# Query stack rows of a pair in a transfer of 48 rows and one of 24, and stack rows dealt to other partitions

## What is computed

```python
q = (x1 @ Wq + bq).reshape(Bn, Nq, H, D).transpose(0, 2, 1, 3)
k = concatenate([x2 @ Wk + bk, memory_k], axis=1)      # 128 + 120 keys
v = concatenate([x2 @ Wv + bv, memory_v], axis=1)
attn = softmax(einsum('bhqd,bhkd->bhqk', q, k) * D ** -0.5)
out = einsum('bhqk,bhkd->bhqd', attn, v)
return x + out.transpose(0, 2, 1, 3).reshape(Bn, Nq, C) @ Wp + bp
```

## Time and profile before

| | us |
|---|---|
| runs of before | 1510.54, 1493.03, 1508.12 |
| median | 1508.12 |
| the profiled execution, its time | 1501.2 |
| its span, first to last instruction | 1499.5 |
| layer 0's attention | some 5 to 540 |
| expert tiles | some 540 to 920 |
| layer 1's attention | some 930 to 1270 |
| adapter | to the end |

### The profile page before, as it was taken

How to read it: one execution, slowest core, us unless ns; L and a number is a source line. 1 busy time by engine, 2 the same in 40 slices (tenths; PEclk the granted TensorE clock), 3 DMA queues, 4 the chain that set the end, 5 groups by cost and what they waited for, 6 DMA issues and landing times. The chain is left out here.

```text
span 1499.5 us, 45714 instructions
## 1 busy us (share of the span) xinstructions
PE 1305.9 (87%) x16549; PEld 1075.4 (72%) x16549; DVE 1078.4 (72%) x3442; ACT 840.7 (56%) x1570; POOL 831.6 (55%) x992
## 2 busy tenths in 40 slices
PE   1799999999999994699999997379999999889998
PEld 0378787778777773699999986157777777666776
DVE  6779989999989975355444444478888788567775
ACT  1267677777777772455555553146666655534444
POOL 4356888888888746466666665345544443022220
PEclk9899999999999996799999999579999999979999
DMA  5666777767777614122222222789998896122221
GB/s 171 222 196 217 238 229 235 233 205 238 231 232 227 211 33 174 54 60 61 57 59 59 61 57 63 182 232 257 253 261 255 256 256 215 60 69 64 75 79 43
DMA packets 183988, 239.26 MB, mean 160 GB/s; under 512 B 37745, under 2 KB 147185, under 8 KB 176609
## 3 DMA queue, kind: packets, MB, share of 16 engines
q1 hardware_dynamic: 164608, 209.51, 45.2%
q0 software_dynamic: 13024, 25.91, 7.1%
q10 hardware_dynamic: 6144, 1.06, 0.4%
HBM read 148.34 MB, written 87.00 MB: 157 GB/s over the span
## 5 line engine op out<-in xcount | busy, mean ns | idle before, releaser
L725 DVE TENSOR_REDUCE L_neg_max<-L_ps_mx 128x2 f32<-128x496 f32 (+1 forms) x768 | 490.0, 659 | 101.1 <-PE L_ps_mx L882 99.0
L592 ACT ACTIVATE L_p<-L_ps_sc 120x512 f32<-120x512 f32 (+1 forms) x768 | 418.2, 598 | 222.1 <-PE L_ps_sc L869 218.1
L882 PE MATMUL L_ps_mx<-stack_k,stack_q 118*128 118x248 bf16 (+1 forms) x2048 | 298.2, 249 | 38.9 <-DMA stack_q<-L_q_rows 25.5
L869 PE MATMUL L_ps_sc<-stack_q,stack_k 122*120 122x128 bf16 (+1 forms) x3072 | 297.8, 220 | 5.6 <-DMA stack_q<-L_mT 5.0
L869 PEld LDWEIGHTS L_ps_sc<-stack_q,stack_k 122*120 122x120 bf16 (+1 forms) x3072 | 237.5, 122 | 55.3 <-issue 35.1
L903 PE MATMUL L_ps_o<-L_p,L_v 120*18 120x128 f32 (+1 forms) x6144 | 218.8, 274 | 1.9 <-ACT L_o_sb L619 1.5
L882 PEld LDWEIGHTS L_ps_mx<-stack_k,stack_q 118*128 118x128 bf16 x2048 | 141.5, 100 | 98.3 <-issue 32.5
L903 PEld LDWEIGHTS L_ps_o<-L_p,L_v 120*18 120x18 f32 (+1 forms) x6144 | 146.8, 97 | 36.7 <-issue 23.0
L1468 DVE TENSOR_TENSOR M_hT<-M_act_a,M_ps_g 128x384 f32<-128x384 f32 x135 | 74.8, 554 | 134.6 <-ACT M_act_a L1442 84.0
L1259 POOL DMA_INDIRECT routed_in<-R_xn,R_slot x128 | 127.2, 994 | 42.1 <-issue 35.8
L1391 POOL DMA_INDIRECT routed_out<-M_y,M_x x135 | 132.1, 978 | 28.6 <-issue 18.6
(11 more groups left out here) (197 smaller groups left out, 2218.8 us busy)
## 6 DMA issues: line engine op xcount, KB each, us to landing
L_q_rows<-L_q_parts_sb SPq DMA_DIRECT2D x192, 192.0 KB, 3.6
stack_q<-L_q_rows SPq DMA_DIRECT2D x192, 192.0 KB
stack_k<-L_k_rows SPq DMA_DIRECT2D x96, 372.0 KB
stack_k<-L_k_rows SPq DMA_DIRECT2D x96, 180.0 KB
L_k_rows<-L_k_parts_sb SPq DMA_DIRECT2D x32, 372.0 KB, 4.2
M_x<-routed_in SPq DMA_DIRECT2D x135, 66.0 KB
x<-L_out SPq DMA_DIRECT2D x32, 256.0 KB, 4.8
L_x<-routed_out POOLq DMA_DIRECT2D x32, 256.0 KB
```

What stands on the lines that cost most here:

```text
L592: nc.scalar.activation(p_t[t][u % 2][:, quarter * 4 * S:(quarter + 1) * 4 * S], ps_sc[n % NSC][0:KEYS[t], :], ACT.Exp).then_inc(sc_read, 1)
L725: nc.vector.tensor_reduce(neg_max[:, b, kk * HPB:(kk + 1) * HPB], v, AX.X, ALU.max, negate=True).then_inc(max_read, 1)
L869: last = mm(ps_sc[n % NSC][0:KEYS[t], j * S:(j + 1) * S], k_st[p][:, b // 2, h, b % 2, k0:k0 + KEYS[t]], q_st[p][:, b // 2, h, b % 2], sta ...
L882: last = mm(ps_mx[i % NMX][:, j * NK:(j + 1) * NK], q_st[p][0:TERM_TOP, b // 2, h, b % 2], k_st[p][0:TERM_TOP, b // 2, h, b % 2], start=Tr ...
```

## The change

The query load of a pair is now two transfers, one of 48 rows that takes blocks 0 and 1 together and one of 24 rows for block 2; the key load stays three transfers of 24 rows. The rows lie on other partitions: blocks 0 and 1 on the even partitions 0 to 94 (block 0 on 0 to 46, block 1 on 48 to 94), block 2 on 1, 5, 9 and so on to 93. `TERM_TOP` falls from 118 to 96, so the max matmul contracts over 96 rows; the rows between hold 0 and ones as before. The waits on `st_loaded` count five transfers for a pair instead of six (`STACK_LOADS`). Nothing else is changed, and the order of the work on PE, ACT, DVE and POOL is the same.

```diff
-ROW_STEP = 5
 BLOCK_ROWS = NPART * DH
-TERM_TOP = ROW_STEP * (BLOCK_ROWS - 1) + NPART
+TERM_TOP = 4 * BLOCK_ROWS
 SHIFT_ROW = 120
+STACK_LOADS = NPART + 2
...
+def stack_rows(part):
+
+    if part == NPART - 1:
+        return slice(1, TERM_TOP, 4)
+    return slice(2 * BLOCK_ROWS * part, 2 * BLOCK_ROWS * (part + 1), 2)
+
+
+FIRST_TWO = slice(0, TERM_TOP, 2)
...
                     if gs.exists:
-                        wait(sp, st_loaded[gs.par][pr], (gs.pair + 1) * 16 * 2 * NPART)
+                        wait(sp, st_loaded[gs.par][pr], (gs.pair + 1) * 16 * STACK_LOADS)
...
                 def load_k(pr):
                     for a in range(NPART):
-                        sp.dma_start(k_st[p][a:TERM_TOP:ROW_STEP, pr].rearrange("r h b s -> r (h b s)"),
+                        sp.dma_start(k_st[p][stack_rows(a), pr].rearrange("r h b s -> r (h b s)"),
                                      k_scr[p, pr].rearrange("c d h b s -> (c d) (h b s)")).then_inc(st_loaded[p][pr], 16)
...
                     wait_apart(sp, q_written[pr], (g2.n + 1) * 16 * NPART, passed)
-                    for a in range(NPART):
-                        sp.dma_start(q_st[p][a:TERM_TOP:ROW_STEP, pr].rearrange("r h b s -> r (h b s)"),
-                                     q_scr[p, pr, a].rearrange("c d h b s -> (c d) (h b s)")).then_inc(st_loaded[p][pr], 16)
+                    for rows, n0, n1 in ((FIRST_TWO, 0, NPART - 1), (stack_rows(NPART - 1), NPART - 1, NPART)):
+                        sp.dma_start(q_st[p][rows, pr].rearrange("r h b s -> r (h b s)"),
+                                     q_scr[p, pr, n0:n1].rearrange("a c d h b s -> (a c d) (h b s)")).then_inc(st_loaded[p][pr], 16)
...
                 if k == 0 and b % 2 == 0:
-                    pe.wait_ge(st_loaded[p][b // 2], (g.pair + 1) * 16 * 2 * NPART)
+                    pe.wait_ge(st_loaded[p][b // 2], (g.pair + 1) * 16 * STACK_LOADS)
```

## The result

The changed kernel takes 1512.14 us (median of 20 runs, 1500.02 to 1523.92), the kernel before on the same chip 1501.90 us (20 runs, 1491.47 to 1510.54). The ratio is 1.0054, with a 95% interval of 1.0033 to 1.0076: slower by about 8 us, where 2 us less was forecast. The ratio leaves out the slowest runs on both sides, so it is smaller than that of the two medians, which lie 10.2 us apart. The profiled execution of after took 1504.19 us (span 1502.5), that of before 1501.2.

The account below looks back on a forecast made before the run. PE was taken as the bound in steady state, busy 97.7 of 100 us in layer 0. Terms -2.0 + 0 + 0 on 1501.2 gave 1499, set to 1503 us from the earlier runs; range 1486 to 1518.

Parts of the forecast that it names:

- What SP is relieved of: SP's query loads: 64 fewer issues, 48-row issue 0.46 us, each pair's load 1.19 us instead of 2.2, gain 1.0 us.
- Rival C: SP's 48-row issue costs 1.4 us, so no gain anywhere: 1505 us; chance 0.15 together with Rival D.
- Start of layer 1: SP's chain of query writes and loads there shortens by two query loads: -2.0 us, ends 0.2 and 2.1.
- Rival D: Start of layer 1: ACT's wait was hidden, so the chain is not shortened: 1505 us; chance 0.15 together with Rival C.
- the steady part: nothing: Steady stretches of both layers: SP does not set the pace, its saved time becomes longer waits; 0 us.
- 96 rows: Max matmuls on PE contract over 96 rows instead of 118: 0 us taken, other end some 55 us faster.
- Start of layer 0: First stack rows and next projection: earlier rows gain nothing overall; 0 us taken, ends -1.0 and +1.5.
- Which partitions the rows go to: Stack loads on more closely packed partitions: 0 us taken, bounds 0 to 1.4 us later per pair.
- Rival B: Crowded partitions make stack loads land later, in layer 0 and then layer 1: +15 us, 26 at most, 1518 us; chance 0.20.
- The cover: Steady state: 1.0 us earlier issue by SP covers most of the 1.4 us per pair that crowded partitions could cost.
- Rival A: Balance over 16 engines shrinks the backlog, shift rows and the starts' input transfers land sooner: 1495 us; chance 0.17.

Follow-up runs that it names:

- packed kernel: Kernel before with all 72 stack rows of a pair side by side on partitions 0 to 71; two runs, ratios to before 1.0192 and 1.0261.
- placement alone: Changed kernel's partitions, but three query loads of 24 rows as before; three runs, ratios to before 1.0053, 1.0056 and 1.0034, mean 1.0048.
- third part high: Changed partitions, but block 2 on 49, 51 to 95, with 48-row transfer or three loads; four ratios to before, mean 1.0015.
- e2: Changed kernel with blocks 0 and 1 moved up 24 partitions, 36 of 72 rows below partition 64; ratio to before 1.0036.
- e8: Kernel before with its three blocks starting at partitions 3, 1, 2 instead of 0, 1, 2; ratio to before 1.0005.
- e2b: Same kernel as e2, in another set of runs; ratio to before 1.0062.
- e12: Changed partitions but block 2 on 49 to 95, three query loads of 24 rows; ratio to before 1.0035.
- e7: Same kernel as e12, on a chip at a clock of 0.95; ratio to before 0.9998.
- e1: Changed kernel's partitions, but three query loads of 24 rows as before; ratio to before 1.0053.
- e1b: Same kernel as e1, in another set of runs; ratio to before 1.0056.
- e10: Same kernel as e1, in a further set of runs; ratio to before 1.0034.
- e0: The changed kernel again, unaltered; ratio to before 1.0002.
- e6: Changed kernel with 48-row transfer kept, but block 2 on partitions 49, 51 to 95; ratio to before 1.0040.
- e11: Same kernel as e6, in another set of runs; ratio to before 0.9988.
- e9: The changed kernel again, unaltered, in another set of runs than e0; ratio to before 1.0039.

## Why the prediction was wrong

- **What SP is relieved of: right, with a part of the reason wrong.** 128 issues came. A query load holds SP 1.31 us where 1.19 was forecast, so 0.9 us were saved and not 1.0; the 48-row issue is 0.53 us, not 0.46. "24 rows seem to be a bad number" was half of it: 24 rows side by side hold SP 0.37 us, so the step between the partitions was the larger part of the 0.70, though at a step of two 24 rows are still dearer than 48. `L_srcT` was the wrong nearest row since it goes to partitions side by side. Rival C (1.4 us) is out. As written, the gain in the steady part became longer waits of SP: at the context load in layer 0 it waits 118.3 us from 100 to 500 us, 106.7 before.
- **Start of layer 1: right.** From the first key write to the end of ACT's second wait it is 44.7 us (947.35 to 992.02) where it was 46.0 (945.40 to 991.44), -1.4 us where -2.0 was forecast; over seven profiles of each form it is -1.7 us, and the first output comes 2.9 us sooner. ACT's second wait fell from 9.56 to 8.62 us. Rival D, that the chain is hidden, doesn't fit the earlier output. But the gain does not reach the end of layer 1: the groups behind lose 2.2 us with the 48-row transfer, which the term "the steady part: nothing" had at 0.
- **96 rows: right**, at 0.
- **Start of layer 0: wrong.** 0 us was taken, with +1.5 as the bad end. PE's first tile came within 0.2 us of before, as written; but by the first output it is 2.3 us later, and the two places that the prediction looked at, the first max tile and the projection behind it, don't hold that.
- **Which partitions the rows go to: the step that failed.** The bounds were 0 to 1.4 us per pair, and I wrote "I take 0, nearest to the row that shows 12 engines at an even 0.74 share". That row shows how many engines are at work. It cannot show how long a row would take elsewhere, since in it all rows are spread; it had nothing to say on the choice. Rival B is what happened, at 0.20, with the first half of its mechanism as written: the engines hold the same bytes longer (occupancy 678 to 706 by placement, a query row's packet 382 to 456 ns). Of the second half, stack rows of layer 0 came late by a little and layer 0 lost 5.6 us; late shift rows are shown for the packed kernel alone. Its price was overstated: 15 us were given as the middle of 0 and 26 with the start added, and about 7 us are measured (0.48% of 1502, placement alone). Its test was half right: shift-row waits over 10 us were to show it, and they are 6.9, while in the packed kernel, where the loss is 37 us (2.3% of 1630), they are 23 to 26. A tell-tale for a rival should be set at the size that the rival would have. The measured 1512 us lies in the stated range only because the range was stretched to B.
- **The cover was misjudged.** "In steady state 1.0 us earlier issue covers most of the other end": SP's earlier issue does come (0.9 us for each query load), and yet PE's waits from 100 to 500 us in layer 0 grow by 3.4 us. Half of that is for the source of the next projection, a transfer that SP issues into the same queue some 3 us behind query rows (at 318.81 us in the group of the earlier trace rows).
- **Rival A** (the balance over 16 engines helps) is out: the shift-row waits went up, not down, and the 48-row form raises the occupancy. Its sign, waits under 1 us, is in no profile.

The Trainium skill's rule (SBUF — State Buffer, "Door 1: The DMA port swizzle") was weighed and not followed. It assigns each partition to one of 16 ports, by which the transfers reach it. Counted by it, the rows that a pair puts on the fullest port are 5 before (no port has 6, as the prediction said of one), 6 on eight ports in the changed partitions and 8 in the packed ones, the order of 678, 706 and 796 to 802 us. The kernels with the third part high have 6 on four ports only and 40 rows, not 48, on the lower half, and 676 to 678 us, level with before. The trace so agrees with the rule in the main order. It doesn't with e2, whose fullest ports, two of them, hold 6 and whose halves are even: 730 and 746 us there, no better than the 721 to 730 of after. Nor does it tell e8 (5, as before) from before, 690 from 678 us. A count over a whole pair is too coarse. That the rows in flight together have to be counted is what e2b's expectation said and its packets bear out; no kernel was built to test it further.

What stays open: whether the 48-row transfer is worth a little or nothing in the whole, since the four pairs contradict each other at 0.5%; why e12, with the occupancy of before, is not as fast; and by what step the start of layer 0 loses its 2.3 us.

## What to carry to other kernels

The partitions that a transfer writes are part of its cost, although bytes, packets and the number of engines are the same: here 72 rows side by side cost about 2% and a milder crowding about 0.5%. Before you call a new placement free, compare what the same bytes cost the engines: the mean time of a packet of each size, or the queue's share times the span. When no row shows an operation, its nearest row must differ in the thing that is in question, or it decides nothing; then the bounds' middle is the honest value, not the end that one would like. Relieving a queue that has slack buys nothing where the waits are for the engines behind it, so count what a change asks of these first. A gain at the start of a stretch is not a gain of the stretch: look at the end of it too.

## What the runs showed of the hardware that was not expected

- Busy share is not throughput. From 100 to 500 us the engines are busy 0.71, 0.73 and 0.79 of the time (e7, before, after) and move 226, 227 and 226 GB/s. In 6 us in which they are 0.91 to 0.93 full the packed kernels move 204 and 210 GB/s, before 245 and e7 300; six us are too short for more, since kernels with one and the same placement read 236 to 252 there (e1, e1b, e10).
- The 48-row form of the same query rows makes the queue occupy the engines 17 to 29 us longer in total, at the same placement (e0 721 against e1 704; e6 702 against e7 676; e11 707 against e12 678; e9 730 against e10 706). It is in the stack rows: a query row's packet takes 498 to 507 ns where it takes 454 to 459 with three transfers. Why is open.
- SP's time for an issue depends on the step between partitions and not on rows or bytes alone: 24 rows 0.37 us with a step of one, 0.70 us with steps of two, four or five; 48 rows with a step of two 0.53 us; 128 rows with a step of one 0.46 us.
- Chips differ. At a granted clock of about 0.91 over the whole program (0.88 to 0.89 from 100 to 500 us, where the faster chips have 1.00) a group of layer 0 takes some 40 us where it takes 32, and the engines' share from 100 to 500 us is 0.62 to 0.63 with the placement alone. Room of that kind should hide the loss, yet placement alone stayed at +0.34 to +0.56% there. In e1b against e8, on one chip, layer 0 ends 6.3 us later, as at full clock, and 3.1 us of it are there at the first output; why the room does not help is open.
